# Decoder layer on one core: an addition moved ahead of a row minimum, a norm and a memset spread over the first pairs, the last two norms moved from GpSimd to VectorE

## The chip, the cores and the metric

The kernel is one program on one core of one Trainium2 chip. The metric is the device time of one execution in microseconds (us). A core has TensorE (PE, with its weight loads shown apart as PEld), VectorE (DVE), ScalarE (ACT), GpSimd (POOL) and the queue of SyncE (SP), which issues the DMAs here.

## The reference

Input `x` is (4, 1024, 256) in f32, `ctx` is (4, 77, 256). Three blocks, each followed by a layer norm without weights over the last axis (256):

```python
# 1: self attention with layer-normed q, k and a sigmoid in place of softmax
scores = layer_norm(q) @ layer_norm(k).T / 16
x = layernorm(x + ((sigmoid(scores - log(1024)) @ v) @ Wo.T + bo) * layerscale)
# 2: cross attention, 16 heads of 16, 77 keys, softmax
x = layernorm(x + softmax(qh @ kh.T / 4) @ vh @ dense_w.T + dense_b)
# 3: feed-forward with a token shift
xk, xr = mu * x + (1 - mu) * x_prev      # x_prev: the row of x before
out = sigmoid(xr @ W_r.T) * (relu(xk @ W_k.T) ** 2 @ W_v.T)
x = layernorm(x + out)
```

## The kernel before

The 4096 rows are 32 tiles of 128 rows; a pair is two tiles (NJ = 16 pairs), a group four (NG = 8). `xs` keeps all rows in SBUF from end to end. Each engine has its own list of calls written out by hand; helpers (`maxima`, `crossed`, ...) each wait on semaphores, issue and signal. An engine works strictly in the order of its list, so a call that waits holds everything behind it on that engine.

Self attention: a loop over 64 steps. The result of a group stands in PSUM (`acc`). For the last group, `attended(7)` on VectorE adds it to `xs`; then `stats1(7)` (L777, L782: mean and variance), `deviation1(7)` on GpSimd (L559, L561: variance + eps, to the power -1/2), and `norm1(7)` on VectorE (L788: four subtract-and-multiply over 128x256, SBUF to SBUF).

Cross attention: the loop over s = 0..18. Step s works on several pairs at once:
- scores and softmax of tiles 2s and 2s+1: `cross_scores` (PE, L1189, two halves of 8 heads), `maxima` (DVE, L826, minimum of negated logits, two halves), `exponentials` (ACT, L381, 32 per tile), `fold_weights` (POOL, L593), `sums` (DVE, L832), `reciprocals` (L839), `normalise` (POOL, L598). For an odd tile the last four come at the start of the next step.
- turning of the weights of tiles 2s-3 and 2s-2: `weights_t` (PE, L1205) in chunks 0, 1, 2 into two alternating PSUM banks; chunks 0 and 1 are copied out by `weights_body` (DVE, L846), chunk 2 by `weights_tail` (ACT, L314 into `pT`). Chunk c waits for the copy of the chunk before the last.
- `mixed(s-2)` (PE, L1222: weights times values into bank `pv_bank`), copied by `mixed_hi` (ACT) and `mixed_lo` (DVE, L708 `oT_lo`).
- `dense(s-3)` (PE, the product of the output projection, into the same `pv_bank`), then `crossed(s-3)` (DVE, L859: adds it to `xs`), `stats2(s-3)` (DVE, L864, L869), `deviation2` (POOL, L607 to L612). `mixed(s-2)` waits for `crossed(s-3)`, since both use `pv_bank`.
- the next queries: `x1(s+2)` (PE transpose), `x1_hi` (ACT), `x1_lo` (DVE, L708 `x1T_lo`), `query(s+2)` (PE, then ACT).
- `residual2` (POOL, L585) adds the bias `bxd` to two tiles of `xs`.

Feed-forward: starts inside s = 16 and runs on over pairs i: `carried` (ACT), `mixes` (DVE), three products on PE, `key_squares_lo(i)` (DVE, L708 `kkT_lo`), `gated(i)` (DVE, L922), `residual3(i)` (POOL, L628), `stats3(i)` (DVE, L929, L934), `norm3(i)` (POOL: L633, L635 for the deviation, L639 twice for the norm), and the output DMA (SP, L305), 256 KB a pair.

`pads()` on GpSimd clears, ahead of the loop, one column in each head of the four weight buffers (four tiny memsets, L569) and the whole third chunk of `pT` (L570), and `fold_weights` of the first tile waits for it.

Of the kernel before, what the change touches and what calls it, by code (L numbers as in the profile page):

```python
# [9 lines left out]
ALU = mybir.AluOpType  # L10
# [32 lines left out]
TY_ONE = 8  # L43

# [26 lines left out]
def decoder_layer(nc, io):  # L71
    ctx = ExitStack()
    with ctx:
# [32 lines left out]
        nlogs = tensor(ctx, "nlogs", [P, 1])  # L106
# [59 lines left out]
        with ExitStack() as ph:  # L166
# [17 lines left out]
        wx_dve, pads_pool = done("wx_dve", 2), done("pads_pool")  # L184
# [15 lines left out]
        fv_pe, fva_dve, fvb_pool, fvs_dve, ln3_pool = (  # L200
            done("fv_pe"), done("fva_dve"), done("fvb_pool"), done("fvs_dve", 4), done("ln3_pool", 4))
# [48 lines left out]
        with nc.Block() as block:  # L250
            @block.sync
            def _(sp):
# [50 lines left out]
                for i in range(NJ):  # L303
                    w.wait_ge(*ln3_pool.at(i))
                    sp.dma_start(out_dram[:, 2 * i:2 * i + 2, :], y[:, i % NY]).then_inc(out_dma[i % NY].sem, 16)  # L305
# [4 lines left out]
            def _(act):  # L310
# [61 lines left out]

                def exponentials(t, e):
                    if t >= NP:
                        w.wait_ge(*tp_pe.at(3 * (t - NP) + 2))
                    else:
                        w.wait_ge(*st_pe.at(NS - 1))
                    for g in (2 * e, 2 * e + 1):
                        w.wait_ge(*mx_dve.at(4 * t + g))
                        for h in range(HG):  # L380
                            ex = act.activation(weights(t)[:, HG * g + h, 0:SC], logits[g][:, h * SC:(h + 1) * SC], ACT.Exp,  # L381
                                                bias=neg_mx[:, t % 2, HG * g + h:HG * g + h + 1], scale=-1.0)
                        ex.then_inc(ex_act.sem, 1)

                def weights_tail(t):
                    w.wait_ge(*tp_pe.at(3 * t + 2))
                    w.wait_ge(*pads_pool.at(0))
# [67 lines left out]
                for u in range(NS // 2):  # L455
# [15 lines left out]
                    if u == 31:  # L471
                        x1_hi(1)
                query(1)
# [41 lines left out]
            def _(pool):  # L515
# [114 lines left out]
                def norm3(i):  # L630
                    w.wait_ge(*fvs_dve.at(i))
                    r = rs3[:, i % 2]
                    pool.tensor_tensor(r, mv3[:, i % 2, :, 1], eps4[:, 0:2], ALU.add).then_inc(ln3_pool.sem, 1)  # L633
                    w.wait_ge(*ln3_pool.at(i, 1))
                    pool.tensor_tensor(r, r, half4[:, 0:2], ALU.pow).then_inc(ln3_pool.sem, 1)  # L635
                    w.wait_ge(*ln3_pool.at(i, 2))
# [37 lines left out]
                deviation1(NG - 1)  # L674
                residual2(1)
                pads()
                for s in range(NJ + 3):
                    if 1 <= s <= NJ:
                        fold_weights(2 * s - 1)
                    if s + 2 < NJ:  # L680
                        residual2(s + 2)
                    if 1 <= s <= NJ:
                        normalise(2 * s - 1)
                    if 0 <= s - 3 < NJ:
                        deviation2(s - 3)
                    if s < NJ:
                        fold_weights(2 * s)
                        normalise(2 * s)
                    for i in (2 * (s - NJ) - 1, 2 * (s - NJ)):
                        if i >= 0:  # L690
# [3 lines left out]
                            if i >= 4:  # L694
                                norm3(i - 4)
                for i in range(5, NJ + 4):
                    if i < NJ:
                        halo(i)
                    if i - 3 < NJ:
                        residual3(i - 3)  # L700
                    norm3(i - 4)

            @block.vector
            def _(dve):
# [220 lines left out]
                def stats3(i):  # L925
                    yy = y[:, i % NY]
                    w.wait_ge(*fvb_pool.at(i))
# [4 lines left out]
                    for t in range(2):  # L932
                        w.wait_ge(*fvs_dve.at(i, 1 + t))
                        dve.bn_aggr(mv3[:, i % 2, t], st3[:, i % 2, t]).then_inc(fvs_dve.sem, 1)  # L934

# [100 lines left out]
                for i in range(5, NJ + 3):  # L1036
                    if i - 1 < NJ:
                        mix_lo(i - 1)
# [3 lines left out]
                    if i - 2 < NJ:  # L1042
                        gated(i - 2)
                    if i - 1 < NJ:
                        key_squares_lo(i - 1)
# [372 lines left out]
```

## Time and profile before

| | |
|---|---|
| median of 3 runs | 629.15 us (626.57 to 630.88) |
| profiled execution | 627.45 us, of which the span is 625.3 us |
| chain that ended last | PE 54%, POOL 15%, DVE 13%, ACT 8%, issue 7% |
| busy share of the span | PE 88%, PEld 73%, DVE 73%, ACT 58%, POOL 56% |
| self attention | to about 301.5 us |
| cross attention | about 301.5 us to 515 us |
| feed-forward | from about 507 us, last norm ends at 622.7 us |

The profiled execution is 2.15 us longer than its span (launch and end). Its time lies within the three runs, 1.7 us under their median. Times of the rows are us from the start of the span; an arrow in brackets tells how long an engine stood idle ahead of an instruction, and what ended that.

### The profile page before, as it was taken

To read this page: it belongs to the slowest core of one execution; us is meant where nothing else is said; L and a number is where in the kernel's file an instruction comes from. 1 tells how busy PE (TensorE), PEld (TensorE's weight loads), DVE (VectorE), ACT (ScalarE), POOL (GpSimd) and SP (SyncE) were. 2 spreads that over 40 slices of the span, in tenths; PEclk is the share of its full clock that TensorE was granted. 3 is DMA by queue.
4 is the path that set the end of the run, shared out by engine and by line. 5 is a ranking of instruction groups with operands and counts; after the bars stand their busy time and mean duration, and the time that the engine had idled before them with its cause. 6 is when DMAs were issued, how large, how long until landed. Compare 5 with 4: busy or idle time off the path is not lost.

```text
span 625.3 us, 11108 instructions
## 1 busy us (share of the span) xinstructions
PE 547.4 (88%) x3952; PEld 455.0 (73%) x3952; DVE 455.0 (73%) x1044; ACT 364.5 (58%) x983; POOL 351.7 (56%) x383
## 2 busy tenths in 40 slices
PE   3879999999999999999569899989989868888981
PEld 2769989898989899878346666666666547788881
DVE  3976566677776676664677888888888867788882
ACT  1245434344444445424378778887888747688871
POOL 3545253434425241514467877878787741688887
PEclk9999999999999999999889999999999999899997
DMA  6221001010130011100000000000000000011111
GB/s 172 67 69 50 20 4 48 18 51 18 50 103 1 1 58 43 52 2 2 0 0 2 1 1 2 2 2 1 3 1 1 2 1 1 35 36 51 45 42 67
DMA packets 18350, 17.53 MB, mean 28 GB/s; under 512 B 1835, under 2 KB 18296, under 8 KB 18296
## 3 DMA queue, kind: packets, MB, share of 16 engines
q1 hardware_dynamic: 18024, 16.57, 8.4%
q8 instruction: 31, 0.51, 0.3%
q10 hardware_dynamic: 272, 0.26, 0.1%
q14 instruction: 23, 0.19, 0.1%
HBM read 12.63 MB, written 4.19 MB: 27 GB/s over the span
## 4 chain that ended last, share of the span: by engine, by line
PE 54%; POOL 15%; DVE 13%; ACT 8%; issue 7%; DMA 1%; SPq 1%; POOLq 0%; DVEq 0%; ACTq 0%
PE ring L213 25%; PE big L213 17%; POOL p_sb L598 5%; POOL fold L593 5%; PE ring L1205 3%; PE ring L1222 2%; PE big L1189 2%; PE ring L1098 2%; ACT p_sb L381 2%; POOL y L639 1%; DVE kkT_lo L708 1%; DMA bo<-in_bo 1%; DVE big L896 1%; DVE st L737 1%; ACT kr L432 1%
## 5 line engine op out<-in xcount | busy, mean ns | idle before, releaser
L381 ACT ACTIVATE p_sb<-big,neg_mx 128x77 f32<-128x77 f32 x384 | 89.6, 346 | 35.7 <-DVE neg_mx L826 35.6
L708 DVE TENSOR_TENSOR aT_lo<-a_sb,aT_hi 128x512 fp32r<-128x512 f32 x64 | 45.5, 712 | 78.9 <-ACT aT_hi L314 78.9
L598 POOL TENSOR_TENSOR p_sb<-p_sb,rc 128x1248 f32<-128x1248 f32 x32 | 73.0, 2282 | 31.0 <-DVE rc L839 31.0
L213 PE MATMUL big<-vv_hi,aT_hi 128*128 128x256 f32 x256 | 72.7, 284 | 3.4 <-DVE xs L772 3.4
L347 ACT ACTIVATE a_sb<-ring,nlogs 128x512 f32<-128x512 f32 x64 | 43.4, 679 | 53.7 <-PE ring L213 53.7
L213 PE MATMUL big<-vv_hi,aT_lo 128*128 128x256 f32 x256 | 72.5, 283 | 0.0
L213 PE MATMUL big<-vv_lo,aT_hi 128*128 128x256 f32 x256 | 72.4, 283 | 0.0
L1205 PE MATMUL ring<-ident,p_sb 128*128 128x128 f32 (+1 forms) x384 | 56.5, 280 | 4.6 <-DVE pT L846 3.0
L1205 PEld LDWEIGHTS ring<-ident,p_sb 128*128 128x128 f32 (+1 forms) x384 | 39.4, 130 | 26.8 <-issue 19.2
L213 PEld LDWEIGHTS big<-vv_hi,aT_hi 128*128 128x128 f32 x256 | 48.8, 191 | 8.1 <-issue 5.8
L1189 PE MATMUL big<-kb,xq 64*128 64x308 f32 x192 | 50.5, 472 | 4.4 <-ACT p_sb L381 3.6
L213 PE MATMUL ring<-qkT_hi 128*128 128x512 f32 x128 | 51.7, 404 | 0.0
L213 PEld LDWEIGHTS big<-vv_lo,aT_hi 128*128 128x128 f32 x256 | 48.8, 191 | 2.2
L213 PE MATMUL ring<-qkT_lo,qkT_hi 128*128 128x512 f32 x128 | 50.2, 392 | 0.0
L213 PE MATMUL ring<-qkT_hi,qkT_lo 128*128 128x512 f32 x128 | 49.9, 390 | 0.0
L537 POOL TENSOR_TENSOR rs<-mv,consts 128x2 f32<-128x2 f32 x32 | 12.5, 389 | 65.9 <-DVE mv L740 65.9
L213 PEld LDWEIGHTS big<-vv_hi,aT_lo 128*128 128x128 f32 x256 | 48.9, 191 | 0.0
L593 POOL TENSOR_TENSOR fold<-p_sb 128x624 f32<-128x624 f32 x32 | 48.7, 1522 | 0.0
L846 DVE COPY pT<-ring 128x512 f32<-128x512 f32 x64 | 43.5, 681 | 4.1 <-PE ring L1205 4.1
L1222 PE MATMUL ring<-pT,vb 128*32 128x256 f32 x512 | 30.9, 381 | 16.7 <-DVE xs L859 15.9
L826 DVE TENSOR_REDUCE neg_mx<-big 128x4 f32<-128x308 f32 x96 | 42.4, 470 | 2.5 <-PE ring L1189 1.8
L547 POOL TENSOR_TENSOR vv_lo<-v_sb,vv_hi 128x512 fp32r<-128x512 f32 x16 | 21.0, 1314 | 40.5 <-ACT vv_hi L314 40.5
(157 smaller groups left out, 1738.0 us busy)
## 6 DMA issues: line engine op xcount, KB each, us to landing
xraw<-in_xT SPq DMA_DIRECT2D x16, 256.0 KB, 2.8
xs<-in_x SPq DMA_DIRECT2D x8, 512.0 KB, 4.1
out_y<-y SPq DMA_DIRECT2D x16, 256.0 KB, 2.1
cT<-in_cT SPq DMA_DIRECT2D x1, 308.0 KB
wraw<-in_wqT ACTq DMA_DIRECT2D x1, 256.0 KB, 3.9
wraw<-in_wkT SPq DMA_DIRECT2D x1, 256.0 KB, 4.5
wv_raw<-in_wv SPq DMA_DIRECT2D x1, 256.0 KB, 5.8
wo_ls<-in_woT SPq DMA_DIRECT2D x1, 256.0 KB, 5.8
```

Source lines behind the costliest of these rows:

```text
L213: mm = pe.matmul(out, s_, m_, start=first and k == 0 and q == 0, stop=last and k == n - 1 and q == 2, skip_group_check=not check)
L347: act.activation(a_sb[:, i % NAR], st_bank[i % 2], ACT.Sigmoid, bias=nlogs[:, 0:1], scale=1.0 / 16).then_inc(st_act.sem, 1)
L381: ex = act.activation(weights(t)[:, HG * g + h, 0:SC], logits[g][:, h * SC:(h + 1) * SC], ACT.Exp, bias=neg_mx[:, t % 2, HG * g + h:HG * g ...
L547: pool.tensor_tensor(lo, tiles(v_sb[:, i % 2]), f(hi), ALU.subtract).then_inc(v_pool.sem, 1)
L593: pool.tensor_tensor(fold[:].rearrange("p (h k) -> p h k", k=FO), p[:, :, 0:FO], p[:, :, FO:2 * FO], ALU.add).then_inc(fo_pool.sem, 1)
L598: pool.tensor_tensor(weights(t), weights(t), rc[:, t % 2].rearrange("p (h o) -> p h o", o=1) .to_broadcast([P, H, SP]), ALU.mult).then_inc ...
L708: return dve.tensor_tensor(lo, whole, f(hi), ALU.subtract)
L826: dve.tensor_reduce(neg_mx[:, t % 2, HG * g:HG * (g + 1)], logits[g][:, 0:LW].rearrange("p (h k) -> p h k", k=SC), AX, ALU.min)\
L846: dve.tensor_copy(pT[:, t // 2 % 2, c, :, (t % 2) * P:(t % 2 + 1) * P], tiles(tp_bank[(3 * t + c) % 2], NH)).then_inc(tp_dve.sem, 1)
L1189: mm = pe.matmul(logits[2 * e + r][:, 0:LW], xq[half, i % 2, e * D + u * P:e * D + (u + 1) * P], kb[half, b, e], start=True, stop=True)
L1205: mm = pe.transpose(tp_bank[n % 2][0:rows, g * P:(g + 1) * P], p_sb[:, t % NP, c0:c0 + rows], ident[:])
L1222: mm = pe.matmul(pv_bank[32 * n:32 * (n + 1), k * D:(k + 1) * D], vb[:, b, kind, g], pT[:, i % 2, c, g], start=first, stop=not first, skip ...
```

## The change

Six edits, all in order or in which engine does a step; the arithmetic stays the same, except that one tiny exponential is added whose result nobody reads.

- (a) VectorE calls `crossed(s-3)` after `weights_body(2s-3, 0)` and ahead of the second half of `maxima(2s)`, where it stood behind `reciprocals(2s-1)`.
- (b) `stats1(7)` moves from ahead of the loop to the end of s = 0, `norm1(7)` into s = 2 (ahead of `weights_body(2s-2, 0)`), `deviation1(7)` on GpSimd into s = 1.
- (c) The big memset of `pT` moves behind `normalise(0)` as `tail_rows()`.
- (d) `residual2(1)` leaves the place ahead of the loop; `residual2(s)` now runs in step s for s = 1..15, where `residual2(s+2)` ran for s = 0..13.
- (e) ScalarE runs one exponential on a spare column ahead of `query(1)`.
- (f) For the last two pairs (NL = 2) the residual addition and the norm run on VectorE; GpSimd keeps the deviation. On VectorE `gated(14)` now stands behind `key_squares_lo(15)`.

```diff
@@ scalar
+                first_exponential()
                 query(1)
@@ gpsimd
                     for n in range(NP):
-                        pool.memset(weights(n)[:, :, SC:SP], 0.0)
-                    pool.memset(pT[:, :, 2], 0.0).then_inc(pads_pool.sem, 1)
+                        own = pool.memset(weights(n)[:, :, SC:SP], 0.0)
+                    own.then_inc(pads_pool.sem, 1)
+
+                def tail_rows():
+                    w.wait_ge(*av_pe.at(NS - 1))
+                    w.wait_ge(*st_dve.at(NS - 1))
+                    pool.memset(pT[:, :, 2], 0.0).then_inc(rows_pool.sem, 1)
...
-                deviation1(NG - 1)
-                residual2(1)
                 pads()
                 for s in range(NJ + 3):
                     if 1 <= s <= NJ:
                         fold_weights(2 * s - 1)
-                    if s + 2 < NJ:
-                        residual2(s + 2)
-                    if 1 <= s <= NJ:
+                        if s < NJ:
+                            residual2(s)
                         normalise(2 * s - 1)
+                    if s == 1:
+                        deviation1(NG - 1)
                     if 0 <= s - 3 < NJ:
                         deviation2(s - 3)
                     if s < NJ:
                         fold_weights(2 * s)
                         normalise(2 * s)
+                    if s == 0:
+                        tail_rows()
...
                 for i in range(5, NJ + 4):
                     if i < NJ:
                         halo(i)
-                    if i - 3 < NJ:
+                    if i - 3 < NJ - NL:
                         residual3(i - 3)
-                    norm3(i - 4)
+                    deviation3(i - 4)
+                    if i - 4 < NJ - NL:
+                        norm3(i - 4)
@@ vector
+                def residual3(i):
+                    w.wait_ge(*fva_dve.at(i))
+                    yy = y[:, i % NY]
+                    dve.tensor_tensor(yy, yy, xs[:, 2 * i:2 * i + 2, :], ALU.add).then_inc(fvb_dve.sem, 1)
+
+                def norm3(i):
+                    w.wait_ge(*ln3s_pool.at(i))
+                    for t in range(2):
+                        yt = y[:, i % NY, t]
+                        dve.tensor_scalar(yt, yt, mv3[:, i % 2, t, 0:1], rs3[:, i % 2, t:t + 1],
+                                          ALU.subtract, ALU.mult).then_inc(ln3_dve.sem, 1)
...
-                stats1(NG - 1)
-                norm1(NG - 1)
                 for s in range(NJ + 3):
                     if 0 < s < NJ:
                         maxima(2 * s, 0)
                     if 0 <= 2 * s - 3 < NT:
                         weights_body(2 * s - 3, 0)
+                    if 0 <= s - 3 < NJ:
+                        crossed(s - 3)
                     if 0 < s < NJ:
                         maxima(2 * s, 1)
                     if 0 <= 2 * s - 3 < NT:
                         weights_body(2 * s - 3, 1)
                     if 1 <= s <= NJ:
                         sums(2 * s - 1)
                         reciprocals(2 * s - 1)
-                    if 0 <= s - 3 < NJ:
-                        crossed(s - 3)
                     if s + 2 < NJ:
                         x1_lo(s + 2)
                     if s < NJ:
                         maxima(2 * s + 1, 0)
+                    if s == 2:
+                        norm1(NG - 1)
                     if 0 <= s - 3 < NJ:
                         stats2(s - 3)
                     if 0 <= 2 * s - 2 < NT:
                         weights_body(2 * s - 2, 0)
                     if 0 <= s - 2 < NJ:
                         mixed_lo(s - 2)
                     if s < NJ:
                         maxima(2 * s + 1, 1)
+                    if s == 0:
+                        stats1(NG - 1)
...
-                    if i - 2 < NJ:
+                    if i - 2 < NJ - NL:
                         gated(i - 2)
-                    if i - 1 < NJ:
-                        key_squares_lo(i - 1)
+                    key_squares_lo(i - 1)
+                for i in (NJ - 2, NJ - 1):
+                    gated(i)
+                    residual3(i)
+                    stats3(i)
+                norm3(NJ - 2)
+                norm3(NJ - 1)
```

## Rows read from the trace of the kernel before

**Rows 1.** The waits, whole span: total, times, longest (us)

```profile
PE ring L1222 <- DVE xs L859: 15.9, 14, 2.6
```

**Rows 2.** Timeline of VectorE, one steady pair: start, duration, what [idle before]

```profile
409.60 0.67 DVE L846 COPY pT<-ring 128x512 f32<-128x512 f32 x1
...
415.89 0.86 DVE L826 TENSOR_REDUCE neg_mx<-big 128x4 f32<-128x308 f32 x2
...
417.74 0.81 DVE L832 TENSOR_REDUCE sm<-fold 128x16 f32<-128x624 f32 x1 [0.38 <-POOL fold L593]
...
418.75 0.63 DVE L859 TENSOR_TENSOR xs<-ring,xs 128x512 f32<-128x512 f32 x1
419.69 0.69 DVE L708 TENSOR_TENSOR x1T_lo<-ring,x1T_hi 128x512 fp32r<-128x512 f32 x1 [0.32 <-ACT x1T_hi L314]
...
421.95 0.67 DVE L846 COPY pT<-ring 128x512 f32<-128x512 f32 x1
```

**Rows 3.** Timeline of ScalarE, TensorE and the weight loads, same pair

```profile
416.91 0.59 ACT L314 ACTIVATE pT<-ring 56x512 f32<-56x512 f32 x1 [0.32 <-PE ring L1205]
417.40 1.78 ACT L381 ACTIVATE p_sb<-big,neg_mx 128x77 f32<-128x77 f32 x8
...
419.52 1.93 PE L1222 MATMUL ring<-pT,vb 128*32 128x256 f32 x32 [0.91 <-DVE xs L859]
...
422.67 0.35 PEld L1205 LDWEIGHTS ring<-ident,p_sb 128*56 128x56 f32 x4 [0.15 <-DVE pT L846]
```

**Rows 4.** Timeline of all engines, from self attention into cross attention

```profile
301.00 1.28 ACT L381 ACT_TABLE_LOAD   x1
303.28 0.97 ACT L381 ACTIVATE p_sb<-big,neg_mx 128x77 f32<-128x77 f32 x4 [0.99 <-DVE neg_mx L826]
...
307.62 6.37 DVE L788 TENSOR_SCALAR xs<-xs,mvl,rsl 128x256 f32<-128x256 f32 x4 [1.41 <-POOL rsl L561]
308.93 1.80 POOL L570 MEMSET pT<- 128x2048 f32 x1
...
311.96 1.55 POOL L593 TENSOR_TENSOR fold<-p_sb 128x624 f32<-128x624 f32 x1
317.20 2.27 POOL L598 TENSOR_TENSOR p_sb<-p_sb,rc 128x1248 f32<-128x1248 f32 x1 [3.69 <-DVE rc L839]
...
327.75 2.27 POOL L598 TENSOR_TENSOR p_sb<-p_sb,rc 128x1248 f32<-128x1248 f32 x1 [1.86 <-DVE rc L839]
...
334.75 0.68 DVE L846 COPY pT<-ring 128x512 f32<-128x512 f32 x1
...
339.97 2.28 POOL L598 TENSOR_TENSOR p_sb<-p_sb,rc 128x1248 f32<-128x1248 f32 x1 [3.53 <-DVE rc L839]
```

**Rows 5.** Instructions of line 788, whole span: ns minimum/median/maximum

```profile
L788 DVE TENSOR_SCALAR xs<-xs,mvl,rsl x32: 399/406/3270, 94.2 to 313.6; 128x256 f32<-128x256 f32 x32
```

**Rows 6.** Timeline of GpSimd and TensorE, end of cross attention

```profile
480.65 2.28 POOL L598 TENSOR_TENSOR p_sb<-p_sb,rc 128x1248 f32<-128x1248 f32 x1 [1.20 <-DVE rc L839]
...
503.93 1.93 PE L1222 MATMUL ring<-pT,vb 128*32 128x256 f32 x32 [2.57 <-DVE xs L859]
...
512.75 1.93 PE L1222 MATMUL ring<-pT,vb 128*32 128x256 f32 x32 [0.73 <-ACT pT L314]
```

**Rows 7.** Timeline of VectorE and GpSimd, end of the kernel

```profile
609.73 1.28 POOL L628 TENSOR_TENSOR y<-y,xs 128x512 f32<-128x512 f32 x1
...
611.04 0.69 DVE L708 TENSOR_TENSOR kkT_lo<-ring,kkT_hi 128x512 fp32r<-128x512 f32 x1 [2.31 <-ACT kkT_hi L442]
...
620.26 2.43 POOL L639 TENSOR_SCALAR y<-y,mv,rs 128x256 f32<-128x256 f32 x2
```

**Rows 8.** Windows: span, busy of each engine (count), granted clock, DMA share, GB/s

```profile
308.00:314.00 6.00, 0.00 (x0) 0.00 (x0) 6.00 (x5) 0.00 (x0) 5.51 (x8) 0.50 0.00 0
```

**Rows 9.** Chain that ended last: start, length, what

```profile
536.11 4.64 PE ring L213 x24
...
594.68 3.14 PE ring L213 x24
```

More of the change, by code:

```diff
@@ L43 @@
 TY_ONE = 8
+NL = 2
 class Done:
@@ L105, in decoder_layer @@
         consts = tensor(ctx, "consts", [P, 12])
-        nlogs = tensor(ctx, "nlogs", [P, 1])
+        nlogs, spare = tensor(ctx, "nlogs", [P, 1]), tensor(ctx, "spare", [P, 1])
         bqcol, bkcol = tensor(ctx, "bqcol", [P, KC]), tensor(ctx, "bkcol", [P, KC])
@@ L183, in decoder_layer @@
             done("xb_pool"), done("ln1a_dve", 2), done("ln1s_dve", 8), done("ln1s_pool", 2), done("ln1b_dve", 4))
-        wx_dve, pads_pool = done("wx_dve", 2), done("pads_pool")
+        wx_dve, pads_pool, rows_pool, ex_table = done("wx_dve", 2), done("pads_pool"), done("rows_pool"), done("ex_table")
         k_pe, k_act, kb_pool = done("k_pe"), done("k_act"), done("kb_pool", 2)
@@ L199, in decoder_layer @@
             done("fr_pe"), done("fr_act"), done("fk_pe"), done("kr_act"), done("kk_act", 2), done("kkl_dve"))
-        fv_pe, fva_dve, fvb_pool, fvs_dve, ln3_pool = (
-            done("fv_pe"), done("fva_dve"), done("fvb_pool"), done("fvs_dve", 4), done("ln3_pool", 4))
+        fv_pe, fva_dve, fvb_pool, fvb_dve, fvs_dve = (
+            done("fv_pe"), done("fva_dve"), done("fvb_pool"), done("fvb_dve"), done("fvs_dve", 4))
+        ln3s_pool, ln3_pool, ln3_dve = done("ln3s_pool", 2), done("ln3_pool", 2), done("ln3_dve", 2)
         out_dma = [done(f"out_dma{n}", 16) for n in range(NY)]
@@ L303, in _ @@
                 for i in range(NJ):
-                    w.wait_ge(*ln3_pool.at(i))
+                    if i < NJ - NL:
+                        w.wait_ge(*ln3_pool.at(i))
+                    else:
+                        w.wait_ge(*ln3_dve.at(i - (NJ - NL)))
                     sp.dma_start(out_dram[:, 2 * i:2 * i + 2, :], y[:, i % NY]).then_inc(out_dma[i % NY].sem, 16)
@@ L371, in query, with first_exponential @@
                         copy(xq[:, i % 2, cut], x_bank[:, cut], bias=bqcol[:, e:e + 1]).then_inc(xq_act.sem, 1)
+                def first_exponential():
+                    act.activation(spare[:], minus4[:, 0:1], ACT.Exp).then_inc(ex_table.sem, 1)
                 def exponentials(t, e):
@@ L386, in weights_tail @@
                     w.wait_ge(*tp_pe.at(3 * t + 2))
-                    w.wait_ge(*pads_pool.at(0))
+                    w.wait_ge(*rows_pool.at(0))
                     if t >= 4:
@@ L628, in residual3, with deviation3 @@
                     pool.tensor_tensor(yy, yy, xs[:, 2 * i:2 * i + 2, :], ALU.add).then_inc(fvb_pool.sem, 1)
-                def norm3(i):
+                def deviation3(i):
                     w.wait_ge(*fvs_dve.at(i))
                     r = rs3[:, i % 2]
[L633 to L636, printed above, removed]
+                    pool.tensor_tensor(r, mv3[:, i % 2, :, 1], eps4[:, 0:2], ALU.add).then_inc(ln3s_pool.sem, 1)
+                    w.wait_ge(*ln3s_pool.at(i, 1))
+                    pool.tensor_tensor(r, r, half4[:, 0:2], ALU.pow).then_inc(ln3s_pool.sem, 1)
+                def norm3(i):
+                    w.wait_ge(*ln3s_pool.at(i))
                     for t in range(2):
@@ L698, in _ @@
                         halo(i)
-                    if i - 3 < NJ:
+                    if i - 3 < NJ - NL:
                         residual3(i - 3)
-                    norm3(i - 4)
+                    deviation3(i - 4)
+                    if i - 4 < NJ - NL:
+                        norm3(i - 4)
             @block.vector
@@ L926, in stats3 @@
                     yy = y[:, i % NY]
-                    w.wait_ge(*fvb_pool.at(i))
+                    if i < NJ - NL:
+                        w.wait_ge(*fvb_pool.at(i))
+                    else:
+                        w.wait_ge(*fvb_dve.at(i - (NJ - NL)))
                     for t in range(2):
@@ L1035, in _ @@
                 norm2(NJ - 1)
-                for i in range(5, NJ + 3):
-                    if i - 1 < NJ:
-                        mix_lo(i - 1)
+                for i in range(5, NJ + 1):
+                    mix_lo(i - 1)
                     stats3(i - 3)
```

3 lines of the change are left out of this document (2 added, 1 removed).

## The prediction

> **What bounds the kernel now.** I read first the chain that ended last with the busy shares. TensorE leads, but not everywhere: in self attention it is dense and the change touches nothing there; at the seam into cross attention, in the last softmax pairs and at the very end the chain runs through VectorE and GpSimd. Then the waits: TensorE stands still 15.9 us, in 14 waits, for the addition of the dense product (L859) [rows 1]. That is the sum that edit (a) aims at. Whether it is worth 15.9 us is to be read from the timeline of one steady pair, engine by engine, because a wait on an engine is worth something only if nothing else ends just after it.
>
> **Edit (a) in the steady pairs: nothing.** A pair takes 12.35 us: the copy of the first chunk starts on VectorE at 409.60 and again at 421.95 [rows 2]. `mixed` starts at 419.52 after 0.91 us of waiting for `crossed` [rows 3]. After it, TensorE does one block of scores and the second chunk, and then the third chunk of the even tile, whose weight load starts at 422.67. And that load also shows a wait, 0.15 us, for the VectorE copy that started at 421.95 and ends at 422.62 [rows 2, 3]. So two waits end one behind the other, and the second is the later one already.
>
> That second wait closes a loop without `mixed` or `crossed` in it: third chunk, query, scores, dense product, first chunk, scores, second and third chunk on TensorE; then ScalarE copies the third chunk (416.91, after 0.32 us waiting for TensorE), does eight exponentials (417.40) and the copy of x1; then VectorE does `x1_lo` (419.69, after 0.32 us waiting for ScalarE), half a `maxima`, `stats2`, and the copy of 421.95 [rows 2, 3]. Each step follows the one before without slack, and the turn is the whole 12.35 us. With `crossed` early, `mixed` starts some 0.9 us sooner and TensorE then stands still about 1.0 us at the third chunk. Gain: 0; bounds: a loss of some 0.05 us a pair if restarting costs, a gain of the 0.91 us if I misread the loop (a rival).
>
> What (a) delays: `crossed` takes 0.55 us from start to next start, in the place of the second half of `maxima` (415.89 becomes 416.4). Behind it are queued that half, one copy and `sums`. The exponentials that read this half start at 417.40, held by the chunk copy, and the first of its two reductions would be done at about 416.85: 0.5 us to spare. `sums` had 0.38 us idle ahead of it and the old place of `crossed` behind it, so it moves by under 0.1 us, and `x1_lo` (0.32 us idle) doesn't move [rows 2, 3]. `crossed` itself never waits there: TensorE does the dense product before the chunk whose copy stands ahead of it.
>
> **Edits (b), (c), (d), (e) at the seam: about -0.8 us.** Now `norm1(7)` takes 6.37 us (307.62 to 313.99) with everything of pair 2 behind it, and the first `normalise` starts only at 317.20 [rows 4]. Yet four such instructions at the median of 0.406 us are 1.6 us [rows 5]. They were slow since GpSimd worked without a pause: the first took 3.27 us, to just behind the end (310.73) of the memset that began at 308.93, and the third ran to just behind the end of the fold (311.96 + 1.55) [rows 4, 5]. One instruction of this kind gets through for each one of GpSimd's. The Trainium skill, "SBUF — State Buffer", section Who interferes with whom, tells of this as an exclusive lock on a port pair that VectorE's two-port modes and GpSimd share; it speaks against part (b), because without it the moved norm would cost 1.6 us.
>
> The new order, with the present durations: `x1_lo(2)` at 307.35, `maxima(1)` to 309.5, `stats1(7)` (1.65) to 311.15, `sums(0)`, reciprocal, `normalise(0)` at 312.3 in place of 317.20: 4.9 us won. Then GpSimd has the memset behind it (1.75), `fold(1)` at 316.25, `residual2(1)` (1.25), `normalise(1)` at 319.0, `deviation1(7)` (1.3), `fold(2)` at 322.5, `normalise(2)` at 325.2 in place of 327.75 [rows 4]: 2.5 us left. In s = 2 VectorE comes to `norm1(7)` at 331.4. GpSimd is then in `normalise(3)` (to 332.4) and `fold(4)` (to 333.95), after which it waits for VectorE. So two of the four wait for GpSimd and two run free: the norm ends at about 334.8, 3.4 us after its start. Behind it is the copy of the first chunk, for which TensorE waits with the query and the whole next step: it stands at 334.75 now [rows 4]. The gain on TensorE's path is thus 0. On the other path `normalise(4)` moves from 339.97 [rows 4] to 338.5, 1.45 us won. In the next pair the two meet: TensorE delivers the third chunk at 342.05, ScalarE was busy until 342.46 and now takes it at once, and down the same steps as in rows 2 and 3 the third chunk of the tile after starts at 347.8 in place of 348.5. Between 0 and 1.45 I take what this gives, 0.7 to 0.8 us. Bounds for (b) as a whole: if the norm ran free (1.6 us), 2.9 us won; if it is held longer, 0.5 us lost.
>
> (e) is worth 0: the table load (1.28 us, from 301.00) is over at 302.28, and the exponentials wait until 303.28 for `neg_mx`, which wait for the last product of self attention [rows 4]. The Trainium skill, "ScalarE: Activation LUTs", What ACT_TABLE_LOAD costs, adds about 1.38 us of draining to a load of this length; that would have ended at 303.66, behind the observed start of the exponentials, so the row shows no such drain, and by the page the early load would win 0.4 us.
>
> (d): `residual2` leaves the seam (counted above) and comes into s = 14 and 15, where the chain is GpSimd's: 1.25 us each. It falls into the 1.20 us that GpSimd waits for a reciprocal there [rows 6]. With `sums` up to 0.1 us late, +0.15 us in all; if that cover failed, +2.5.
>
> **Edit (a) at the end of cross attention: -1.6 us.** In s = 16 there is no query or score left, and `mixed(14)` at 503.93 has waited 2.57 us for `crossed(13)` [rows 6], which stood behind a `sums` that waits for GpSimd. Ahead of it, `mixed(14)` can start at 501.3 (after the chunk of tile 30, normalised at 500.65). What is late next: the first copy of tile 30 on VectorE, behind that same `sums` and `stats2`, starting 504.0 in place of 504.7; then its third chunk on TensorE, the transpose for the feed-forward at 505.3 in place of 506.7, and so on to `mixed(15)` at 511.15 in place of 512.75 [rows 6]. 1.6 us, bounds 0.7 and 2.6.
>
> **Edit (f): -3.7 us.** At the end GpSimd works alone without a pause from residual3(14) at 609.73 to the end of norm3(15), 620.26 + 2.43 = 622.69, and norm3(14) takes part in it [rows 7]. New: VectorE is free at 611.65, after `kkT_lo` of pair 15 [rows 7]; `gated(14)` to 612.25; its residual reads two SBUF tiles and may be held by norm3(13) on GpSimd (to about 613.2), ending 613.7; stats to 614.65; `gated(15)` 615.2; residual 615.85 (0.69 as the same shape in rows 7); stats 616.75; norm3(14), 0.75 us, while GpSimd does the deviation of pair 15 to 618.15; norm3(15), 0.75, to 618.95. 622.69 - 618.95 = 3.7. Bounds 3.0 (each wait for the port full) and 4.3 (none). The last DMA takes what it takes now, 2.6 us to the end of the span.
>
> **Sum.** 0 - 0.8 + 0.15 - 1.6 - 3.7 = -5.95 us. The profiled execution's 627.45 becomes 621.5; scaled by 629.15/627.45 to the median, 623.2, 0.95% less. About 1% is what a measurement of this kernel can tell from no change, so this stands right at the edge.
>
> **Rivals.**
> 1. The 0.91 us does come out of each steady pair: the loop through the third chunk is not tight. Ten pairs, 9.2 us more: 614. For it: the 15.9 us [rows 1]. Against: the 0.15 us wait that stands behind it [rows 3]. 8%.
> 2. Slower: `crossed` ahead of the second half of `maxima` holds the exponentials of s, which are in the loop. It decides once that half's first reduction ends after 417.4, that is with over 0.5 us more delay than I count. Its full price is 0.55 us for each of 14 pairs, +7.7: 627.45 - 5.95 + 7.7 = 629.2, as a median 630.9. 5%.
> 3. TensorE's clock. With TensorE idle, the granted clock was 0.50 from 308 to 314 [rows 8], half of 2.4 GHz, and 24 multiplications near 536 took 4.64 us in place of 3.14 [rows 9]. In the new seam TensorE idles more often in short pieces (about 3.5 us in s = 1 and again in s = 2), ahead of a stretch where it counts. One more such stretch costs 1.5 to 4.6 us (three times the 1.5): 624.7 to 627.8. 15%.
> 4. The moved norm is not held by GpSimd (it takes the port first, or falls into a gap): 2.1 us more, 621.1. 10%.
>
> **How the numbers follow.** My forecast has 62%, own range 621 to 625.5 from the bounds of (b), (a) and (f). The range for 8 in 10 takes in rivals 3 and 4 and some of the run to run spread of 0.3%: 618.5 to 627.6. It leaves out rivals 1 and 2. Faster by over 1% means below 622.9: rivals 1 and 4 and somewhat over four tenths of the forecast, 0.44. Slower by over 1%, above 635.4, would need rival 2 with 3: 0.04. The rest, 0.52.
>
> **What would show it.** In the profile after: the pair still takes 12.35 us; the waits for L859 are gone and L1205 waits for the copy of the first chunk, about 1 us a pair; the four L788 of group 7 take about 3.4 us near s = 2; mixed(15) starts about 2.3 us earlier than now; the last norm ends 3.7 us closer to mixed(15). A pair of 11.5 us is rival 1, one near 12.9 rival 2, a second stretch at 0.50 ahead of 345 us rival 3.

## The result and the profile after

| | before | changed |
|---|---|---|
| median | 630.01 us (626.57 to 630.88, 4 runs) | 620.78 us (620.12 to 622.19, 4 runs) |
| ratio of the two, 95% interval | | 0.9867 (0.9823 to 0.9910) |
| profiled execution, its span | 627.45, 625.3 | 621.29, 619.2 |

The change makes the kernel 1.3% faster by the ratio, where 0.95% was forecast. The profiled executions differ by 6.16 us, where the prediction's sum was 5.95.

To see where the difference arises, both traces are laid over each other at the same instructions. Times in this table are us from the start of `attended(7)` on VectorE (301.57 in the trace before, 301.24 after), read from the timelines; "stats2(n)" is the start of its first instruction, "mixed", "kkT_lo" and "last norm" likewise.

| | before | after | the gap grows by |
|---|---|---|---|
| stats2(0) | 45.10 | 47.13 | +2.03 |
| stats2(10) | 168.90 | 170.75 | -0.18 |
| normalise(31) | 201.74 | 203.29 | -0.30 |
| mixed(15) | 211.18 | 211.17 | -1.56 |
| kkT_lo(3) | 241.03 | 239.58 | -1.44 |
| kkT_lo(15) | 309.47 | 307.95 | -0.07 |
| last norm | 321.12 | 315.34 | -4.26 |
| end of span | 323.73 | 317.96 | +0.01 |

With the 0.33 us that `attended(7)` starts earlier, the last column adds up to the 6.1 us between the spans. So the new seam loses time, the steady pairs give nothing, and the end of cross attention, the start of the feed-forward and the tail win.

**Steady pairs.** The waits of the changed kernel (total, times, longest, us) no longer list one for the addition, now L879. In place of [rows 1] stands a wait for the copy of a chunk, L866:

```profile
PE ring L1246 <- DVE pT L866: 20.4, 19, 3.2
```

Timeline of VectorE, one pair of the changed kernel, which answers to [rows 2]:

```profile
435.77 0.67 DVE L866 COPY pT<-ring 128x512 f32<-128x512 f32 x1
...
441.95 0.68 DVE L879 TENSOR_TENSOR xs<-ring,xs 128x512 f32<-128x512 f32 x1
442.55 0.85 DVE L846 TENSOR_REDUCE neg_mx<-big 128x4 f32<-128x308 f32 x2
...
445.88 0.69 DVE L728 TENSOR_TENSOR x1T_lo<-ring,x1T_hi 128x512 fp32r<-128x512 f32 x1 [0.86 <-ACT x1T_hi L319]
...
448.14 0.67 DVE L866 COPY pT<-ring 128x512 f32<-128x512 f32 x1
```

And TensorE with ScalarE in the pair, which answers to [rows 3]:

```profile
430.72 0.59 ACT L319 ACTIVATE pT<-ring 56x512 f32<-56x512 f32 x1 [0.29 <-PE ring L1246]
431.21 1.79 ACT L389 ACTIVATE p_sb<-big,neg_mx 128x77 f32<-128x77 f32 x8
...
432.35 1.93 PE L1263 MATMUL ring<-pT,vb 128*32 128x256 f32 x32
...
436.50 0.62 PE L1246 MATMUL ring<-ident,p_sb 128*56 128x128 f32 x4 [0.90 <-DVE pT L866]
```

`mixed` follows without idle time, where it had waited 0.91 us, and TensorE stands still 0.90 us at the third chunk of the even tile instead. The copy comes every 12.37 us (435.77, 448.14). The wait has only moved down the loop.

**Seam.** All engines but TensorE's, which answers to [rows 4]:

```profile
296.14 1.28 ACT L379 ACT_TABLE_LOAD   x1
...
311.91 2.28 POOL L612 TENSOR_TENSOR p_sb<-p_sb,rc 128x1248 f32<-128x1248 f32 x1 [3.81 <-DVE rc L859]
314.13 1.81 POOL L584 MEMSET pT<- 128x2048 f32 x1
...
324.84 2.28 POOL L612 TENSOR_TENSOR p_sb<-p_sb,rc 128x1248 f32<-128x1248 f32 x1 [1.20 <-DVE rc L859]
...
331.25 3.13 DVE L808 TENSOR_SCALAR xs<-xs,mvl,rsl 128x256 f32<-128x256 f32 x4
334.30 0.68 DVE L866 COPY pT<-ring 128x512 f32<-128x512 f32 x1
...
338.02 2.28 POOL L612 TENSOR_TENSOR p_sb<-p_sb,rc 128x1248 f32<-128x1248 f32 x1 [4.44 <-DVE rc L859]
340.03 0.48 DVE L846 TENSOR_REDUCE neg_mx<-big 128x4 f32<-128x308 f32 x1 [2.08 <-PE ring L1230]
```

Take 0.33 us off the forecast's times, since the seam starts that much earlier, and every step stands where the prediction put it: normalise(0) at 311.91 (312.0), normalise(2) at 324.84 (324.9), the norm of the last group at 331.25 (331.1) with 3.13 us (3.4), the copy behind it at 334.30 (334.5), normalise(4) at 338.02 (338.2). But the last row shows something that was not in the sum: VectorE then waits 2.08 us for scores. TensorE in the same stretch:

```profile
320.50 1.05 PE L1246 MATMUL ring<-ident,p_sb 128*56 128x128 f32 x4 [3.17 <-DVE pT L866]
...
335.04 1.05 PE L1246 MATMUL ring<-ident,p_sb 128*56 128x128 f32 x4 [3.08 <-DVE pT L866]
...
336.10 0.41 PE L215 MATMUL ring<-x1T_lo,wx_hi 128*128 128x256 f32 x1
...
338.58 0.88 PE L1230 MATMUL big<-kb,xq 64*128 64x308 f32 x1
```

and the windows (length, busy time and count of PE, PEld, DVE, ACT, POOL, then the granted clock, DMA share and GB/s):

```profile
320.00:322.00 2.00, 1.50 (x8) 1.38 (x9) 1.81 (x4) 2.00 (x12) 1.92 (x3) 0.58 0.00 0
...
334.00:336.00 2.00, 0.96 (x5) 0.83 (x6) 2.00 (x6) 0.00 (x1) 0.00 (x0) 0.50 0.01 4
336.00:338.00 2.00, 2.00 (x11) 2.00 (x11) 1.91 (x4) 2.00 (x9) 0.00 (x0) 0.50 0.00 0
338.00:340.00 2.00, 2.00 (x9) 0.95 (x7) 0.00 (x0) 1.12 (x3) 1.98 (x1) 0.50 0.00 0
...
518.00:520.00 2.00, 2.00 (x13) 2.00 (x12) 0.95 (x3) 1.54 (x3) 0.00 (x0) 0.57 0.00 0
...
534.00:540.00 6.00, 4.76 (x38) 4.55 (x39) 6.00 (x15) 3.99 (x9) 4.52 (x5) 1.00 0.00 0
```

The granted clock is 0.50 (1.2 GHz of 2.4) at 308 to 310, about 320 to 324, and 334 to 341. The second and third follow pieces of 3.17 and 3.08 us in which TensorE waited for a copy. The twelve multiplications of the query then take 0.41 us each in place of 0.28, start every 0.21 us in place of 0.12, and the scores behind them come late. That is rival 3. Before, the clock was low at 308 to 318, and TensorE stood idle for the first 6 us of it [rows 8]. That is one trace: e2 below has the same order of the seam as the kernel before and loses as much there as the changed kernel. The last two lines show the other side: the low stretch that the kernel before had at 536 [rows 9] is gone (1.00), and the one at 518 costs next to nothing: mixed(15) to kkT_lo(3) takes 28.41 us here and 28.30 in e6, which has no low stretch there.

**End of cross attention and tail.** GpSimd, TensorE and VectorE, which answer to [rows 6] and [rows 7]:

```profile
480.94 1.27 POOL L599 TENSOR_TENSOR xs<-xs,bxd 128x512 f32<-128x512 f32 x1
...
502.49 1.93 PE L1263 MATMUL ring<-pT,vb 128*32 128x256 f32 x32
...
512.41 1.93 PE L1263 MATMUL ring<-pT,vb 128*32 128x256 f32 x32 [0.73 <-ACT pT L319]
...
608.98 2.43 POOL L655 TENSOR_SCALAR y<-y,mv,rs 128x256 f32<-128x256 f32 x2
609.19 0.69 DVE L728 TENSOR_TENSOR kkT_lo<-ring,kkT_hi 128x512 fp32r<-128x512 f32 x1 [2.93 <-ACT kkT_hi L450]
...
610.52 0.77 DVE L962 TENSOR_TENSOR y<-y,xs 128x512 f32<-128x512 f32 x1
...
612.95 0.69 DVE L962 TENSOR_TENSOR y<-y,xs 128x512 f32<-128x512 f32 x1
...
615.85 0.73 DVE L968 TENSOR_SCALAR y<-y,mv,rs 128x256 f32<-128x256 f32 x2 [0.59 <-POOL rs L649]
```

The moved residual (480.94) fills what was a 1.20 us wait. `mixed(14)` has no idle time ahead of it, and `mixed(15)` comes 7.88 us behind normalise(31) in place of 9.44. In the tail the first residual on VectorE runs beside the norm on GpSimd (608.98 to 611.41) in 0.77 us, hardly longer than the 0.69 us of the second one, beside which GpSimd works only on the two numbers a row of the deviation: it was not held.

### The profile page after: what moved, and what is told of

Same layout as the page of the kernel before. It is cut to its first block, busy times and chain, and to the rows that moved or that the text cites. A ratio compares the mean times of both kernels' runs of the same rounds, so it can differ in the third digit from the quotient of the medians.

```text
span 619.2 us, 11109 instructions
## 1 busy us (share of the span) xinstructions
PE 551.2 (89%) x3952; PEld 455.2 (74%) x3952; DVE 453.1 (73%) x1050; ACT 366.4 (59%) x984; POOL 344.9 (56%) x377
## 4 chain that ended last, share of the span: by engine, by line
PE 58%; DVE 15%; ACT 12%; POOL 6%; issue 5%; DMA 1%; SPq 1%; POOLq 0%; DVEq 0%; ACTq 0%
PE ring L215 29%; PE big L215 17%; PE ring L1246 4%; ACT p_sb L389 4%; PE big L1230 3%; POOL p_sb L612 2%; PE ring L1139 2%; DVE neg_mx L846 2%; POOL fold L607 2%; DVE pT L866 2%; DVE kkT_lo L728 1%; DVE st L884 1%; ACT kr L440 1%; ACT kkT_hi L450 1%; ACT pT L319 1%
## 5 line engine op out<-in xcount | busy, mean ns | idle before, releaser
L1246 PE MATMUL ring<-ident,p_sb 128*128 128x128 f32 (+1 forms) x384 | 58.7, 283 | 21.8 <-DVE pT L866 20.4
L866 DVE COPY pT<-ring 128x512 f32<-128x512 f32 x64 | 43.6, 681 | 5.0 <-PE ring L1246 5.0
L319 ACT ACTIVATE xT_hi<-xraw 128x512 fp32r<-128x512 f32 x16 | 10.1, 631 | 55.7 <-PE big L215 50.0
```

Of the source, the lines that this page charges most:

```text
L319: return act.activation(out, in_, ACT.Identity, **kw)
L866: dve.tensor_copy(pT[:, t // 2 % 2, c, :, (t % 2) * P:(t % 2 + 1) * P], tiles(tp_bank[(3 * t + c) % 2], NH)).then_inc(tp_dve.sem, 1)
L1246: mm = pe.transpose(tp_bank[n % 2][0:rows, g * P:(g + 1) * P], p_sb[:, t % NP, c0:c0 + rows], ident[:])
```

## The experiments

The theory was: (a) is worth nothing in the steady pairs and 1.6 us at s = 16 and 17; (f) is worth some 4.2 us; the seam edits do what was forecast, 0.8 us won, but for the clock, which takes 2.6 us back. The rivals: (a) does pay in the pairs; the loss at the seam comes from the order on the engines (the norm or the memset in the wrong place), not from the clock.

All ratios are against the kernel before, with 95% intervals. The first four kernels ran on one chip beside 22 runs of the kernel before (median 630.84 us, 627.92 to 633.28), the other four beside 11 runs (631.04, 627.48 to 633.51). Beside the medians stand the times at the same instructions in the trace of each:

| us from attended(7) | stats2(0) | stats2(10) | normalise(31) | mixed(15) | kkT_lo(3) | kkT_lo(15) | last norm |
|---|---|---|---|---|---|---|---|
| before | 45.10 | 168.90 | 201.74 | 211.18 | 241.03 | 309.47 | 321.12 |
| changed | 47.13 | 170.75 | 203.29 | 211.17 | 239.58 | 307.95 | 315.34 |
| e1, (a) alone | 45.48 | 169.06 | 201.59 | 209.46 | 240.44 | 308.84 | 320.49 |
| e2, (f) alone | 46.86 | 170.70 | 203.57 | 214.64 | 245.48 | 313.86 | 321.26 |
| e3, seam alone | 45.87 | 169.42 | 202.29 | 213.35 | 244.13 | 312.54 | 324.22 |
| e4, TensorE busy | 44.58 | 168.13 | 200.68 | 208.56 | 239.46 | 307.84 | 315.21 |
| e5, changed again | 47.19 | 170.68 | 203.20 | 211.08 | 241.55 | 309.91 | 317.29 |
| e6, memset early | 44.28 | 167.76 | 200.27 | 208.15 | 236.45 | 304.83 | 312.21 |
| e7, norm by tile | 41.89 | 166.97 | 199.49 | 207.36 | 237.84 | 306.22 | 313.58 |
| e8, e6 and e7 | 40.23 | 165.39 | 197.91 | 205.78 | 234.69 | 303.04 | 310.40 |

**e1, the addition alone.** The kernel before with edit (a) only.

```diff
                     if 0 <= 2 * s - 3 < NT:
                         weights_body(2 * s - 3, 0)
+                    if 0 <= s - 3 < NJ:
+                        crossed(s - 3)
...
-                    if 0 <= s - 3 < NJ:
-                        crossed(s - 3)
```

> The kernel before with edit (a) alone. My reading (the loop through the third chunk sets the pair, so the early addition wins only where scores and queries are over, in s = 16 and 17): the steady pair stays at 12.35 us, the waits of TensorE for the addition go and about 0.9 us a pair of waiting for the copy of the first chunk comes; the time falls by 1 to 2 us, 0.2 to 0.3%. Rival (the wait was worth what it showed): a pair of 11.5 us and 10 to 15 us less.

Measured: 625.20 us (623.91 to 628.56), ratio 0.9931 (0.9910 to 0.9952). The pair stays what it was (copies of the first chunk on VectorE; the last line is mixed(14), forecast for 501.3):

```profile
409.83 0.67 DVE L846 COPY pT<-ring 128x512 f32<-128x512 f32 x1
...
422.19 0.67 DVE L846 COPY pT<-ring 128x512 f32<-128x512 f32 x1
...
501.24 1.93 PE L1222 MATMUL ring<-pT,vb 128*32 128x256 f32 x32
```

12.36 us from one to the next: (a) pays nothing in the pairs, and the rival falls. Its gain by the ratio, 0.7% or 4.4 us, is more than the forecast's 1.6 us and the 1 to 2 us expected here. Part of the rest is visible: from normalise(31) to mixed(15) this kernel takes 7.87 us and every kernel with (a) about 7.9; without (a) it is 9.44 in the profiled run of before, but 11.07 in e2 and 11.06 in e3, both with a stretch of half clock there. So in these traces (a) is worth 1.6 us at full clock and 3.2 us where the clock falls behind its waits. Another 0.3 us comes ahead of that, from stats2(10) to normalise(31). The other 1 us or so is not accounted for; the profiled run is one of the longer ones of e1 (626.96 us).

**e2, the last norms alone.** Edit (f) on the kernel before, the rest as before.

```diff
+                for i in (NJ - 2, NJ - 1):
+                    gated(i)
+                    residual3(i)
+                    stats3(i)
+                norm3(NJ - 2)
+                norm3(NJ - 1)
```

> The kernel before with edit (f) alone. From the profile after: from the last kkT_lo on VectorE to the end of the last norm 7.4 us in place of 11.65, so 4.2 us less, 0.65 to 0.7%. Rival (the forecast's size, with the residual of pair 14 held by GpSimd): 3.7 us less. If the end of the kernel gains only together with the early addition, under 2 us.

Measured: 626.38 us (623.43 to 627.22), ratio 0.9936 (0.9914 to 0.9959), 4.0 us by the ratio. From kkT_lo(15) to the last norm 7.40 us, where before has 11.65 and the changed kernel 7.39. The tail is a piece of its own, worth 4.25 us.

This trace shows something else. Its seam has the order of the kernel before, and yet it reaches stats2(10) at 170.70, 1.80 us later than the profiled run of before and as late as the changed kernel (170.75). It has a low stretch that the profiled run of before does not have:

```profile
326.00:328.00 2.00, 2.00 (x11) 2.00 (x11) 1.44 (x3) 2.00 (x10) 0.44 (x1) 0.50 0.00 0
```

Of the three traces with the old order here, two stand near 169.0 at stats2(10) (before, e1) and one at 170.70; of the three with the new order and nothing added, two at 170.7 (the changed kernel, e5) and one at 169.42 (e3). The means are 0.7 us apart. So a single pair of traces says little about what the new order costs; e3's runs say more.

**e3, the seam alone.** Edits (b), (c) and (d), without (a), (e) and (f). Of the edit, what VectorE's list shows:

```diff
-                stats1(NG - 1)
-                norm1(NG - 1)
...
+                    if s == 2:
+                        norm1(NG - 1)
...
+                    if s == 0:
+                        stats1(NG - 1)
```

> The kernel before with edits (b), (c) and (d) alone: norm, deviation and memset of the seam spread, without the early addition, the early exponential and the last norms. The changed kernel's profile reaches the first stats2 2.0 us later than before, counted from the addition of the last group, and I put this down to (b) to (d) together with TensorE's clock. If so, this kernel is 1 to 2 us slower than before. Rival (the forecast, and the loss comes from the early addition or from chance): 0.8 us faster.

Measured: 631.42 us (629.94 to 633.24), ratio 1.0014 (0.9998 to 1.0030): 0.9 us slower by the ratio, and the rival's 0.8 us faster (0.9987) lies outside the interval. The reordering gives no gain by itself. On GpSimd it follows the changed kernel within 0.1 us as far as normalise(4) (36.79 us from attended(7), 36.78 there), and it has a stretch at 0.50 behind the gap in s = 2 too, a shorter one (0.77 at 334 to 336, 0.50 to 338, 0.88 to 340); that its stats2(0) comes 1.26 us sooner is thus not the order either. Without (e) its first exponential starts 1.70 us behind attended(7), with (e) in the changed kernel 1.71: (e) is worth nothing here. The three parts, which leave out (e), multiply to 0.9931 x 0.9936 x 1.0014 = 0.9881, within the intervals of the whole (0.9867, and 0.9874 in e5).

**e4, TensorE kept busy.** The changed kernel with 25 multiplications (128x128 by 256 columns, `keep_busy`) ahead of the third chunk in s = 1 and 26 in s = 2, whose results nobody reads, so that TensorE does not stand idle there. Nothing else is altered.

```diff
+                        if s == 1:
+                            w.wait_ge(*st_act.at(NS - 1, 1))
+                            keep_busy(pv_bank, 25)
+                        if s == 2:
+                            w.wait_ge(*tx_dve.at(4))
+                            keep_busy(x_bank, 26)
```

> The changed kernel with 51 extra multiplications whose results nobody reads, in the two gaps of about 3.2 us in which TensorE waits for the copy of the first chunk (s = 1 and s = 2). Theory (the seam lost its gain since the granted clock fell to half behind these gaps: query and scores behind them took twice as long): the stretches at 0.50 near 320 and 334 us go, the first stats2 comes about 2.5 us earlier, and the time is 2 to 2.5 us under the changed kernel. Rival (the clock falls all the same, or VectorE and GpSimd set this stretch): no change, or up to 1 us slower for the extra work.

TensorE at both places, and the windows:

```profile
318.62 3.55 PE L1330 MATMUL ring<-wx_hi 128*128 128x256 f32 x25
...
331.75 3.35 PE L1330 MATMUL ring<-wx_hi 128*128 128x256 f32 x26
334.99 0.62 PE L1246 MATMUL ring<-ident,p_sb 128*56 128x128 f32 x4
...
336.98 0.52 PE L1230 MATMUL big<-kb,xq 64*128 64x308 f32 x1
```

```profile
312.00:318.00 6.00, 5.36 (x21) 2.56 (x18) 1.98 (x5) 4.31 (x19) 6.00 (x4) 0.54 0.00 0
318.00:324.00 6.00, 6.00 (x47) 5.86 (x47) 4.10 (x10) 3.97 (x17) 5.48 (x5) 0.89 0.01 3
...
336.00:342.00 6.00, 6.00 (x47) 4.69 (x46) 4.81 (x11) 5.07 (x20) 4.02 (x3) 1.00 0.01 3
```

VectorE and GpSimd do what they do in the changed kernel, at the same times (the norm from 331.29 in 3.05 us), up to the scores behind the second gap.

In s = 1 the extra work wins nothing. The clock was at half until about 319 (0.54 from 312 to 318), the extra work took longer than the gap, and the third chunk starts at 322.00 where the changed kernel has 320.50. The query behind it then ran at full clock, and the scores start at 323.96, against 323.93. What the low stretch in s = 1 costs this run doesn't show.

In s = 2 the third chunk is as early as in the changed kernel (334.99 against 335.04). But at full clock the scores start at 336.98 in place of 338.58, and stats2(0) comes 2.55 us sooner than in the changed kernel, 0.52 us sooner than before; at stats2(10) it is 0.77 us sooner than before. That is the 0.8 us of the forecast, which was worked out from that same trace of before. Only what TensorE does in its gaps was altered, so between these traces it is the clock behind the second gap that turned 0.8 us won into 1.85 lost, and not the order on the engines.

The runs don't show the 2 to 2.5 us that were expected under the changed kernel: the median is 621.11 us (619.03 to 621.62), the ratio 0.9850 (0.9828 to 0.9872), and its interval overlaps those of the changed kernel (0.9867, and 0.9874 in e5). The profiled run has a low stretch further on (kkT_lo(3) is 30.9 us behind mixed(15), where the changed kernel has 28.4).

**e5, the changed kernel again**, beside the next three.

> The changed kernel unaltered, on the same chip as the three beside it, so that they can be compared with it run for run. Theory (the time of one kernel varies by how often TensorE's clock falls to half and where): its runs spread over 2 to 4 us, the longer ones with the lower mean granted clock; ratio near the first one, 0.987.

Measured: 621.78 us (620.81 to 625.28), ratio 0.9874 (0.9843 to 0.9905). Its trace shows the same two gaps and the same price:

```profile
322.36 1.06 PE L1246 MATMUL ring<-ident,p_sb 128*56 128x128 f32 x4 [3.20 <-DVE pT L866]
336.89 1.06 PE L1246 MATMUL ring<-ident,p_sb 128*56 128x128 f32 x4 [2.98 <-DVE pT L866]
```

**e6, the memset early.** The changed kernel with (c) undone: the memset again ahead of the loop, where GpSimd waits for the exponentials anyway.

```diff
                 pads()
+                tail_rows()
...
-                    if s == 0:
-                        tail_rows()
```

> The changed kernel with edit (c) undone: the memset of the third chunk stands ahead of the loop again, where GpSimd is idle for 4.7 us (301.9 to 306.6). Theory (GpSimd's line normalise, memset, fold sets s = 1 and s = 2): fold(1) starts 1.8 us earlier, and so do normalise(1) and the norm of the last group; up to 1.8 us less at the first stats2, less where the clock falls. Rival (the copy behind the norm sets it, and the norm only waits longer for GpSimd): no gain.

GpSimd:

```profile
302.09 1.81 POOL L584 MEMSET pT<- 128x2048 f32 x1
306.88 1.51 POOL L607 TENSOR_TENSOR fold<-p_sb 128x624 f32<-128x624 f32 x1 [2.99 <-ACT p_sb L389]
...
314.43 1.51 POOL L607 TENSOR_TENSOR fold<-p_sb 128x624 f32<-128x624 f32 x1
```

Measured: 619.99 us (618.58 to 621.31), ratio 0.9834 (0.9808 to 0.9860), and stats2(0) at 44.28 in place of 47.13. The runs of e5 (620.81 to 625.28) and of this kernel overlap only at their edges, though the intervals of the ratios overlap. Part (c), read as a part of the changed kernel, is then most likely a loss: once the norm has left this place, GpSimd waits ahead of the first fold, and even behind the memset 2.99 us of that wait are left. Behind normalise(0) it delays fold(1): 315.89 in the changed kernel, 14.65 us from attended(7), where it is 12.89 here. The 2.85 us in the table is that delay and one low stretch fewer: TensorE's gap in s = 1 is shorter (1.45 us), and from 318 to 324 this kernel's granted clock is 1.00.

**e7, the norm tile by tile.** The changed kernel, with the four subtract-and-multiply instructions of the norm called one at a time, in s = 1 to 4, behind the reciprocal of the even tile, when GpSimd stands waiting for that very reciprocal.

```diff
+                def norm1_tile(g, t):
+                    w.wait_ge(*ln1s_pool.at(g))
+                    x1 = xs[:, 4 * g + t]
+                    dve.tensor_scalar(x1, x1, mvl[:, t, 0:1], rsl[:, t:t + 1],
+                                      ALU.subtract, ALU.mult).then_inc(ln1b_dve.sem, 1)
...
-                    if s == 2:
-                        norm1(NG - 1)
...
+                    if 1 <= s <= 4:
+                        norm1_tile(NG - 1, s - 1)
```

> The changed kernel with the norm of the last group cut in four: one tile of 128x256 behind the reciprocal of the even tile in s = 1 to 4, where GpSimd waits for that reciprocal and the port is free. Theory (3.1 us of norm in one piece keep the chunk copy, and TensorE idle behind it, and the clock falls): each of the four takes 0.3 to 0.4 us, the copy of s = 2 starts 2.5 to 3 us earlier, the stretch at half clock near 334 us goes, and the time is 1.5 to 4 us under the changed kernel. Rival (GpSimd's line sets the seam in any case): under 0.5 us.

VectorE:

```profile
325.19 0.32 DVE L815 TENSOR_SCALAR xs<-xs,mvl,rsl 128x256 f32<-128x256 f32 x1
...
331.77 0.68 DVE L872 COPY pT<-ring 128x512 f32<-128x512 f32 x1
```

Measured: 619.84 us (617.96 to 620.33), ratio 0.9824 (0.9798 to 0.9850); its slowest run is faster than the fastest of e5. A tile takes 0.32 us instead of 0.78, and the copy that TensorE waits for comes at 331.77 in place of 334.30; stats2(0) is at 41.89, 5.2 us sooner than in the changed kernel. The gap at s = 2 is gone, and with it the low stretch behind it: the other way of taking the gap away, and the same answer as e4. By stats2(10) 3.78 of the 5.2 us are left: one pair, from stats2(1) to stats2(2), takes 13.92 us at full clock (13.96 in e8), and no run takes that apart.

**e8, both.** e6 and e7 in one kernel, the version that the runs point to.

> The changed kernel with the early memset and the norm cut in four together. Theory: both lines, GpSimd's and VectorE's, are shortened, so the gains add, 3 to 5 us under the changed kernel, ratio to before near 0.980. Rival: no more than the better one of the two alone.

Measured: 618.75 us (615.88 to 620.33), ratio 0.9815 (0.9782 to 0.9848): 12.3 us under the kernel before, 3.0 under the changed one beside it. Against e6 and e7 alone (619.99, 619.84) the intervals overlap, so the times don't decide between theory and rival. In the traces the gains add in part: at stats2(10) e6 is 2.99 us ahead of the changed kernel, e7 3.78, e8 5.36. The windows across the seam:

```profile
306.00:312.00 6.00, 4.47 (x20) 3.27 (x20) 4.68 (x15) 4.86 (x22) 1.51 (x1) 0.72 0.00 0
312.00:318.00 6.00, 4.14 (x24) 2.16 (x24) 3.68 (x10) 4.65 (x20) 5.84 (x4) 1.00 0.00 0
318.00:324.00 6.00, 4.66 (x32) 3.28 (x32) 4.11 (x10) 4.76 (x20) 4.72 (x5) 1.00 0.00 0
```

Of the three low stretches of the changed kernel's seam, one is left.

## Why the prediction was right

It forecast 623.2 us as a median and 621.5 for the profiled run; 620.78 and 621.29 came. The sum for the profiled run was right to 0.2 us, and that is luck in good part. The seam came out 2.65 us worse than forecast. The start of the feed-forward (1.44), (f) (0.56), the stretch ahead of normalise(31) (0.45) and the 0.33 us that self attention, which the change does not touch, was shorter in this run made up for it.

| term | forecast | measured | |
|---|---|---|---|
| (a), steady pairs | 0 | +0.12 | stats2(1) to stats2(10), counted in the next row too; e1: +0.09 |
| seam, (b) to (e) | -0.8 | +1.85 | -0.77 with the gaps filled (e4) |
| (d) at s = 14, 15 | +0.15 | +0.03 | e3, with (d) and without (a) |
| (a) ahead of normalise(31) | not in it | -0.31 | e1, with (a) and without (d); the changed kernel, with both: -0.30 |
| (a) at s = 16, 17 | -1.6 | -1.56 | e1: 7.87 us |
| start of the feed-forward | not in it | -1.44 | a low stretch of before is gone |
| (f) | -3.7 | -4.26 | e2: -4.25 |

- **The steady pairs.** The step that mattered most for the outcome held: in the steady pairs the waits of [rows 1] are worth nothing, since a second wait ends behind the first [rows 3]. What was named in advance, some 1 us of waiting for the copy, is there at 0.90 us. Rival 1 is out, and so is rival 2: `crossed` takes nothing from the exponentials (they start 0.49 us behind the chunk copy on ScalarE, as before). Rival 4, a norm that GpSimd does not hold, is out too: 3.13 us for four where they take 1.6 us unhindered. (Rival 1's ten pairs of 0.91 us are 9.1 us and not 9.2, and three times 1.5 in rival 3 is 4.5 and not 4.6; neither changes anything.)
- **The seam.** The mis-sized term is "about -0.8 us". Every start on VectorE and GpSimd came within 0.2 us, and the norm held by GpSimd took 3.13 us for 3.4. What failed is the assumption beside it, that TensorE would work at full clock; the prediction had this as rival 3, at 15%, with the price of 1.5 to 4.6 us for a further low stretch. It happened, at 2.6 us. It should have been given more than 15%: the text itself counted two idle pieces of 3.5 us, and before's own rows show the half clock with TensorE idle [rows 8] and, in longer multiplications, over dense work [rows 9]. Over many runs the loss is smaller than in this pair of traces: e3's runs put the seam at 0.9 us slower (-0.1 to +1.9).
- **The start of the feed-forward.** The low stretch that made 24 multiplications take 4.64 us [rows 9] was in the trace, but the sum took it as fixed. In the changed kernel it lies elsewhere. That this was a gain here is chance, and e5's trace of the same kernel shows it: there kkT_lo(3) comes 30.5 us behind mixed(15), not 28.4.
- **(a) and (d) at the end of cross attention.** -1.6 forecast for (a) at s = 16 and 17, -1.56 measured. The gain of 0.3 us ahead of it was not in the sum; it is (a)'s, since e1 has it without (d), and (d) itself costs nothing that shows.
- **(f).** Too small by 0.56 us, since the prediction let the first residual on VectorE be held by GpSimd's norm (to 613.7, some 1.45 us) and it took 0.77.
- **The signs named in advance.** The pair of 12.37 us, the wait that moved to the chunk copy (0.90 us) and the norm of 3.13 us came as named, and so did the sign of rival 3, a second stretch at 0.50 ahead of 345 us. Two did not: mixed(15) was to start 2.3 us earlier and starts 0.34 us earlier (512.41 for 512.75), and the last norm was to end 3.7 us closer to mixed(15) and ends 5.77 closer (1.44, 0.07 and 4.26).
- **The median.** It came 2.4 us below the forecast. 629.15 stood for before on three runs; more runs of it give medians of 630.0 to 631.0, and the profiled execution of before was one of its quickest. This is why the medians differ by 9 us and the traces by 6.

## What to carry to other kernels

Before counting a wait as a gain, walk the loop of one steady period and look for the wait that ends next; 0.15 us on the following instruction was enough to show that 0.91 us in each steady pair is worth nothing. When an edit shifts where TensorE idles, cost the clock as well: the gap of 3.08 us at s = 2, with the query and the scores behind it, cost 2.55 us between the traces of the changed kernel and e4. And of an engine that blocks another (the norm on VectorE against GpSimd), place each single instruction where the other is waiting for you anyway, instead of moving the block as a whole (e7, 1.9 us under the same kernel by the medians). And take more than one trace of the kernel before: two traces with the same order of the seam (before and e2) lie 1.8 us apart there, more than the term that was forecast.

## What was not expected of the hardware

- Where the half clock falls moves a run by nearly as much as the largest edits here. The same changed kernel had its low stretches of the granted clock in different places in two profiled runs, 619.2 and 623.1 us long; over the 11 runs of e1, those with a mean clock of 0.983 or 0.986 took 623.9 to 625.2 us, those with 0.975 to 0.978 627.0 to 628.6.
- An addition on VectorE of two SBUF tiles ran beside a subtract-and-multiply on GpSimd (608.98 to 611.41) in 0.77 us, where the subtract-and-multiply on VectorE was held (3.13 us for four beside GpSimd, 0.32 us for one while GpSimd waits). The Trainium skill, "SBUF — State Buffer", Who interferes with whom, says that a VectorE instruction with two SBUF inputs contends with a GpSimd one that reads SBUF. For the subtract-and-multiply the trace agrees with the exclusive lock that the section describes; for this addition it does not, and the measurement decides. But it is not so for every pair: in self attention of the same trace a subtraction on VectorE with two SBUF inputs took 1.96 us in place of the usual 0.69, and ended behind the addition on GpSimd beside it. What sets the two cases apart isn't shown; GpSimd's instruction read two full tiles here, and one tile with two numbers a row in the tail.

```profile
251.21 2.40 POOL L562 TENSOR_TENSOR xs<-xs,bo 128x1024 f32<-128x1024 f32 x1
252.21 1.96 DVE L728 TENSOR_TENSOR aT_lo<-a_sb,aT_hi 128x512 fp32r<-128x512 f32 x1 [2.11 <-ACT aT_hi L319]
```

- The table load at 296.14 ended at 297.42 and the next ScalarE instruction, the spare exponential, started at 297.44: no drain is visible behind it in this trace either, nor ahead of it (the copy before it ends at 296.13).
